# Relation pass of a graph network: SP fetches one chunk in 64 row by row, GpSimd the others without the padding

## What is computed

```python
# layer 1 (relation pass), h = layernorm(x)
msg = h[edge_src] * edge_norm[:, None]
agg = segment_sum(msg, edge_rel * N + edge_dst)          # 8 relations
out = einsum('rnbi,rbio->nbo', agg, W)                   # 8 blocks of 32 x 32
# layer 3 (attention pass)
alpha = leaky_relu(a_src[src] + a_dst[dst]); w = softmax of alpha over each dst
out = segment_sum(xp[src] * w, dst)
```

## Time and profile before

| | |
|---|---|
| median of 3 runs | 7745.9 us (7744.19 to 7753.85) |
| the profiled execution | 7754.0 us |
| its span, first to last instruction | 7752.0 us |
| stage 1 (up to the first gather) | 0 to 387.5 us |
| relation pass, first gather to last add | 387.5 to 2943.5 us |
| attention pass, first to last gather | 3668.7 to 6536.6 us |
| mean granted clock of PE over the span | 0.716 of full speed |

### The profile page before, as it was taken

How to read it: one execution, slowest core, us unless ns; L and a number is a source line. 1 busy time by engine, 2 the same in 40 slices (tenths; PEclk the granted TensorE clock), 3 DMA queues, 4 the chain that set the end, 5 groups by cost and what they waited for, 6 DMA issues and landing times. The chain is left out here.

```text
span 7752.0 us, 114430 instructions
## 1 busy us (share of the span) xinstructions
PE 5127.6 (66%) x25073; PEld 4291.3 (55%) x25073; DVE 4010.3 (52%) x11854; ACT 1970.2 (25%) x4898; POOL 4204.7 (54%) x4656
## 2 busy tenths in 40 slices
PE   9935555555555558697355656565655656769999
PEld 4424455454545546596344445454544545659998
DVE  5534444444444448523555555555555556764443
ACT  3300000000000005232232333332322333436666
POOL 1166666666666655355655555555555554654444
PEclk9967666666666679798566666666556566559999
DMA  8833333333333327112432333333333332644444
GB/s 310 314 91 87 88 87 87 87 87 87 87 87 87 87 78 241 66 63 88 117 87 78 88 87 82 87 86 82 86 82 82 84 86 66 200 147 71 71 71 67
DMA packets 378112, 797.65 MB, mean 103 GB/s; under 512 B 88994, under 2 KB 234994, under 8 KB 364692
## 3 DMA queue, kind: packets, MB, share of 16 engines
q0 software_dynamic: 209712, 525.20, 26.1%
q1 hardware_dynamic: 140724, 154.25, 6.4%
q10 hardware_dynamic: 27440, 116.02, 4.0%
HBM read 565.73 MB, written 229.43 MB: 103 GB/s over the span
## 5 line engine op out<-in xcount | busy, mean ns | idle before, releaser
L1274 POOL DMA_INDIRECT s_rows<-xp_table,s_index x1664 | 1593.2, 957 | 1276.0 <-DVE s_scaled L1562 768.1
L1397 PE MATMUL s_part<-s_pick,s_scaled 128*128 128x128 f32 x6656 | 1603.9, 404 | 949.5 <-DVE s_scaled L1562 650.4
L373 PE MATMUL s_part<-s_pick,s_rows 128*128 128x128 f32 x6656 | 1444.8, 382 | 1114.5 <-DVE s_pick L381 685.4
L347 POOL DMA_INDIRECT s_rows<-rel_table,s_staged x1664 | 1580.7, 950 | 929.6 <-issue 432.6
L1397 PEld LDWEIGHTS s_part<-s_pick,s_scaled 128*128 128x128 f32 x6656 | 1330.7, 289 | 1187.8 <-DVE sums L1577 681.4
L373 PEld LDWEIGHTS s_part<-s_pick,s_rows 128*128 128x128 f32 x6656 | 1231.6, 270 | 1328.3 <-DVE s_pick L381 818.5
L394 DVE TENSOR_TENSOR sums<-sums,s_part 128x256 f32 x1666 | 702.6, 422 | 1237.8 <-issue 689.8
L1577 DVE SCALAR_TENSOR_TENSOR sums<-sums,s_old_share,s_part 128x256 f32 x1666 | 795.6, 478 | 1051.1 <-DMA s_rows<-rel_table,s_staged 540.1
L1310 ACT ACTIVATE s_apart<-window,s_local 128x128 f32<-128x128 f32 x1664 | 531.6, 390 | 1854.7 <-PE s_part L1397 1362.8
L1562 DVE TENSOR_TENSOR s_scaled<-s_rows,s_psW 128x256 f32<-128x256 f32 x1664 | 678.5, 408 | 69.7 <-issue 69.7
L381 DVE TENSOR_SCALAR s_pick<-window,s_local,s_weight 128x128 f32<-128x128 f32 x1669 | 595.4, 357 | 157.3 <-issue 105.5
(11 more groups left out here) (356 smaller groups left out, 5423.2 us busy)
## 6 DMA issues: line engine op xcount, KB each, us to landing
rel_table<-s_rows ACTq DMA_DIRECT2D x98, 1024.0 KB
s_rows<-exp_rows SPq DMA_DIRECT2D x212, 132.0 KB
s_rows<-rel_table,s_staged POOLq DMA_INDIRECT x1664
s_rows<-xp_table,s_index POOLq DMA_INDIRECT x1664
s_edges<-edge_rows SPq DMA_DIRECT2D x208, 80.0 KB
xp_table<-s_xp ACTq DMA_DIRECT2D x49, 264.0 KB, 3.9
s_x<-in_x SPq DMA_DIRECT2D x98, 128.0 KB
s_x<-in_x SPq DMA_DIRECT2D x49, 256.0 KB
```

The source lines that it names most:

```text
L347: pool.indirect_dma_start(out=rows[:, s, :], out_offset=None, in_=rel_table[:, :], in_offset=bass.IndirectOffsetOnAxis(ap=staged[:, 2 * s ...
L373: mm = pe.matmul(part[s % PARTS][:, k, :], rows[:, s, k * P:(k + 1) * P], pick[:, s % PICKS, :], start=True, stop=True)
L1274: pool.indirect_dma_start(out=rows[:, b * BATCH + s, :], out_offset=None, in_=xp_table[0:NR, :], in_offset=bass.IndirectOffsetOnAxis(ap=in ...
L1397: mm = pe.matmul(part[s % 4][:, k, :], scaled[:, s % SCALED, k * P:(k + 1) * P], pick[:, s % (2 * GRP), :], start=True, stop=True)
```

## The change

SP gets slot 63 of every round. To have its row numbers in order, stage 1 copies every 64th column of `index` (26 of them) on DVE, PE transposes them, DVE copies them to `lists`; SP stores these to memory (`fetch_lists`) at the begin of the pass. For a round SP loads one list of 128 numbers to one partition (`list_now`), waits until PE has used slot 63 of the round before, reads the numbers into registers, four to a load, and issues for each a transfer of one row of 1 KB to its partition: 32 loads and 128 transfers a round. The rows count on two semaphores in turn, and PE waits for both at slot 63. The list of the next round is loaded after the last register load of this one.

POOL leaves out slot 63, and of the last round the chunks from 1661 on (slots 61 and 62), and in the attention pass the three padding chunks. For this the last round of POOL and PE and the last iteration of POOL in the attention pass are written out behind their loops.

```diff
+FILLED = -(-E // P)
+FOUR = 4
@@ stage 1, DVE, at the end
+                    def own_chunks():
+                        v.wait_ge(edges_done, 1)
+                        v.tensor_copy(own[:, :], index[:, SLOTS - 1:CHUNKS:SLOTS]).then_inc(own_ready, 1)
...
+                    v.wait_ge(own_turned, 1)
+                    v.tensor_copy(lists[:, :], psI[0:CHUNKS // SLOTS, :])
@@ stage 1, PE, at the end
+                    pe.wait_ge(own_ready, 1)
+                    pe.transpose(psI[0:CHUNKS // SLOTS, :], own[:, :], ident[:, :]).then_inc(own_turned, 1)
@@ relation pass, SP: new
+                    def load_list(i):
+                        sp.dma_start(list_now[:, :], fetch_lists[ds(i, 1), :]).then_inc(list_in, 16)
+
+                    def fetch(i, more):
+                        sp.wait_ge(list_in, 16 * i + 16)
+                        sp.sem_inc(fetch_go, 1)
+                        for j in range(0, P, FOUR):
+                            _, from_rows = nc.values_load_multi_w_load_instructions(
+                                list_now[0:1, j:j + FOUR], engines=[mybir.EngineType.SP], min_val=0, max_val=R * NR - 1,
+                                skip_runtime_bounds_check_because="a source times eight plus a type, both in range")
+                            if more and j + FOUR == P:
+                                load_list(i + 1)
+                            for k, from_row in enumerate(from_rows):
+                                sp.dma_start(rows[j + k:j + k + 1, SLOTS - 1, :], rel_table[ds(from_row, 1), :]).then_inc(fetched[k % 2], 16)
+
+                    sp.dma_start(fetch_lists, lists[:, :]).then_inc(lists_out, 16)
+                    sp.wait_ge(lists_out, 16)
+                    load_list(0)
+                    fetch(0, True)
+                    with sp.Fori(1, ROUNDS2 - 1) as i:
+                        sp.wait_ge(product, SLOTS * i + 2)
+                        fetch(i, True)
+                    sp.wait_ge(product, SLOTS * (ROUNDS2 - 1) + 2)
+                    fetch(ROUNDS2 - 1, False)
@@ relation pass, ACT
-                                act.wait_ge(gathered[g], 16 * GRP * i)
+                                act.wait_ge(gathered[g], 16 * (GRP if g < GROUPS - 1 else GRP - 1) * i)
@@ relation pass, POOL
+                            if s == SLOTS - 1 or isinstance(i, int) and i * SLOTS + s >= FILLED:
+                                continue
@@ relation pass, PE
-                                pe.wait_ge(gathered[s // GRP], 16 * GRP * i + 16 * GRP)
+                                by_pool = GRP if s + GRP < SLOTS else GRP - 1
+                                pad = max(0, c + by_pool - FILLED) if isinstance(i, int) else 0
+                                pe.wait_ge(gathered[s // GRP], 16 * by_pool * i + 16 * (by_pool - pad))
+                            if s == SLOTS - 1:
+                                for k in range(2):
+                                    pe.wait_ge(fetched[k], 16 * P // 2 * i + 16 * P // 2)
@@ attention pass, POOL
-                                gather(s, b)
+                                if not isinstance(i, int) or (2 * i + b) * BATCH + s < FILLED:
+                                    gather(s, b)
@@ attention pass, ACT
-                        act.wait_ge(gathered[b], LANDED * i + LANDED)
+                        pad = max(0, (2 * i + b + 1) * BATCH - FILLED) if isinstance(i, int) else 0
+                        act.wait_ge(gathered[b], LANDED * i + LANDED - 16 * pad)
```

More of the change, by code:

```diff
@@ L93, in gnn_kernel @@
     edge_rows = dram("edge_rows", [CHUNKS, 5, P])
+    fetch_lists = dram("fetch_lists", [CHUNKS // SLOTS, P], I32)
     whole_rows = dram("whole_rows", [BATCHES, HEADS * BATCH])
@@ L160, in gnn_kernel @@
         local = at(gather_of, "s2_local", [P, CHUNKS + AHEAD])
+        lists = at(gather_of, "s2_lists", [CHUNKS // SLOTS, P], I32)
         weight = at(gather_of, "s2_weight", [P, CHUNKS + AHEAD])
@@ L175, in gnn_kernel @@
             psT = [bank(st, f"s1_psT{b}", HALVES, P) for b in range(2)]
+            psI = bank(st, "s1_psI", P)
+            own = at(st, "s1_own", [P, CHUNKS // SLOTS])
+            own_ready, own_turned = sem("s1_own_ready"), sem("s1_own_turned")
             psO = [bank(st, f"s1_psO{k}", R * P, banks=2) for k in range(HALVES)]
@@ L261, in step @@
                             pair_nodes()
+                            own_chunks()
                     norm(0, 0, 0)
                     by_tiles(v, step)
+                    v.wait_ge(own_turned, 1)
+                    v.tensor_copy(lists[:, :], psI[0:CHUNKS // SLOTS, :])
                 @block.scalar
@@ L315, in gnn_kernel @@
             pick = at(st, "s2_pick", [P, PICKS, P])
+            list_now = at(st, "s2_list_now", [1, P], I32)
+            lists_out, list_in, fetch_go = sem("s2_lists_out"), sem("s2_list_in"), sem("s2_fetch_go")
+            fetched = [sem(f"s2_fetched{k}") for k in range(2)]
             part = [bank(st, f"s2_part{k}", HALVES, P) for k in range(PARTS)]
@@ L324, in gnn_kernel, with _ @@
             with nc.Block() as block:
+                @block.sync
+                def _(sp):
+                    def load_list(i):
[20 more added lines that the diff above has]
+                    fetch(ROUNDS2 - 1, False)
                 @block.scalar
@@ L355, in _, with later_round @@
                             gathers(0, g, True)
-                    with pool.Fori(1, ROUNDS2) as i:
+                    def later_round(i):
                         for b in range(2):
@@ L360, in _, with combine_round @@
                                 gathers(i, g, False)
+                    with pool.Fori(1, ROUNDS2 - 1) as i:
+                        later_round(i)
+                    later_round(ROUNDS2 - 1)
                 @block.tensor
                 def _(pe):
-                    pe.sem_inc(product, 2)
-                    with pe.Fori(0, ROUNDS2) as i:
+                    def combine_round(i):
                         for s in range(SLOTS):
@@ L375, in _ @@
                             mm.then_inc(product, 1)
+                    pe.sem_inc(product, 2)
+                    with pe.Fori(0, ROUNDS2 - 1) as i:
+                        combine_round(i)
+                    combine_round(ROUNDS2 - 1)
                 @block.vector
@@ L1297, in _ @@
                         gather(s, 1)
-                    with pool.Fori(1, BATCHES // 2) as i:
+                    with pool.Fori(1, BATCHES // 2 - 1) as i:
                         gathers(i, 0)
                         gathers(i, 1)
+                    gathers(BATCHES // 2 - 1, 0)
+                    gathers(BATCHES // 2 - 1, 1)
                 @block.scalar
```

## The result

The kernel after takes 8566.2 us (median of 4 runs, 8544.6 to 8587.1) against 7745.4 us before (4 runs): a ratio of 1.1056, interval 1.1043 to 1.1069, 821 us slower. The forecast was 7726 us with a range up to 8150. The profiled execution of the kernel after took 8587.1 us, that of before 7754.0.

What follows compares the result with a forecast made beforehand. It took the relation pass to be paced by POOL's gather runs slowing DVE's queue, then POOL pausing at a full ring. Terms -31 + 13 + 0 - 2 = -20 us from 7745.9 gave 7726 us, range 7700 to 8150.

Steps and rivals of the forecast that it cites:

- Fewer gathers, 31 us: Relation pass: POOL's omitted gathers save 1.25 us in each of 25 rounds, 31 us; bounds 0 and 42 us.
- SP's chain, 73 us a round: Relation pass: SP's 32 groups of one four-number load and four row transfers take 2.29 us each; bounds 70 and 113.
- Rival 2: Register loads on SP cost number by number: 7741 us at 2.75 us per four rows (0.06), 7980 at 3.2 (0.10).
- The cover, 96.5 us: Relation pass: SP's chain plus landing, 75 us, hides within a whole round of 96.5 us, with 20 to spare.
- Rival 1: Relation pass: slow stretches beside gathers hit SP's queue too, +11 us a round, 8036 us; chance 0.31.
- The share 0.46: Relation pass: DVE's queue is slow for 46% of the time, from 0.93 us a chunk fast, 5.1 slow, 1.50 mean.
- The last round, +13 us: Relation pass: the last round's cover is only 62 us, so 13 us of SP's chain and landing are paid.
- The first round free: Relation pass: SP's first fetch costs nothing, starting about 395 us while PE reaches the round's end at 561.7 us.
- DMA, 0: Relation pass: 128 more descriptors a round on SP's queue replace a gather of the same bytes; engines 31% busy, cost nothing.
- Stage 1, 0: Before the relation pass: the added copies and transpose hide in 5 us of cover; zero, or 1 us without it.
- Attention pass, -2: Attention pass: three padding gathers fewer count only in the last batch, saving 0 to 3.8 us, taken as 2.
- Rival 3: Relation pass: POOL's saved time was idle anyway and becomes pause, leaving the last round's 13 us, 7757 us; chance 0.06.

## Why the prediction was wrong

*Fewer gathers, 31 us.* Right in its mechanism, a little small: 1.6 us a round in the run with the slot left out, over the upper bound of 1.50; the forecast took 1.25. On the second kind of chip, where POOL is the bound, 28 gathers fewer at 1.25 give 35 us; 37 were measured.

*SP's chain, 73 us a round.* Right in itself: 72.5 us in the last round, 2.27 us for four rows instead of 2.29. The parts were off and made up for each other: the load 555 ns instead of 268 and the 152 of what waits for it, the transfer 225 instead of 260. Rival 2 (7741 or 7980 us) is out.

*The cover, 96.5 us, "75 us fit with 20 to spare".* This step failed. It set the duration of a chain whose queue runs undisturbed against a stretch in which gathers run. Beside them the chain needs 125.7 us and PE stands 32.6 us a round, where the forecast had no wait before the last round.

*Rival 1.* The mechanism is this one, at +11 us a round and 8036 us; it was +33.4. The step that was mis-sized is the rate of 0.66 = 0.54 + 0.46/3.7. The share 0.46 was worked out from DVE's chunks, and taken over for SP. By the rows of the kernel after: PE waits 32.6 us of the 129.9, and POOL stands still then too; less 2 for the landing, SP works 30 us there at its full speed (in the tenth of the later rounds POOL's last gather starts at 1849.7 us, and the trace has none of SP's slow instructions from 1852 to the end of the chain at 1880.6). So it did 72.5 - 30 = 42 us of its work in the other 95, a rate of 0.45. With the slow stretch 3.7 times as long that would be a slow share of 0.75, an estimate. DVE's chunk is in good part work of its engine, which the stretches don't touch; SP's chain is queue instructions and nothing else, and its own chain lengthens DVE's stretches too. The range's end of 8150 us varied the chain by 5 us and left the rate alone. The rate's own bound, slow all the time, is 1/3.7 = 0.27: 26 us of work done beside gathers, 46 left over, a round of 143 us and some 8900 us, which would have held the result.

*The last round, +13 us.* Right for PE, from 62.2 us to 75.8, but only 8 of it reach the end of the pass: before, DVE's last add came 6 us after PE's last matmul (2945.3 against 2939.2 us), and now it comes less than 1 us after (3777.6 against 3776.9). *The first round free.* Wrong: it ends 22 us later. POOL fills the empty ring, 123 gathers in the first 203 us, and SP needs 191 us for its first chain (390.2 to 581.3 us).

*DMA, 0.* Nothing speaks against it. *Stage 1, 0.* Right: the first gather starts at 387.6 us against 387.5. *Attention pass, -2.* It doesn't show: what lies behind the last add is 4806.7 us before and 4807.8 after, and on the second kind of chip 4024.4 after and 4022.3 to 4027.0 in the four kernels with all gathers. *Rival 3* is out.

*The chance.* The forecast gave the mechanism that decided 0.31 and its own 0.42; slower it had at 0.46 in all and faster at 0.36, so its number, that of the likeliest single case, lay on the less likely side. Against rival 1 stood that the queues of PE and ACT show no such stretch. That is true, and for PE it stayed true. It was no witness for another queue in new work, as the run with ACT showed.

*What stays open:* what it is in a gather that holds up the queues of other engines, and why two chips are free of it. Shown is: it takes gathers by POOL (plain loads at a higher DMA share don't do it); it hits SP, DVE in the relation pass and ACT when it fetches, not PE, nor ACT in the attention pass; it depends on the gathers' pace and on what else the queues issue; and the chips differ in it with the same program. A rule of the Trainium skill (Perfetto Trace Analysis, DMA Optimizations) says that balancing transfers across the engines that can issue them may help where the bottleneck is making descriptors. On the second kind of chip, where POOL with its gathers is the bound, the measurement agrees, 0.57% faster. On the first POOL is not the bound, it waits for PE, so the rule's condition isn't met, and the same move costs 10.6%.

## What to carry to other kernels

An engine that seems idle is not free: before a chain of small instructions is put on its queue, look in the trace for the maxima of such instructions on any queue beside the same neighbours, and price the whole chain at the slow rate as the bound. Another queue that stays fast there is no witness that this one will: ACT's was fast beside gathers in one pass and slow when it fetched rows in the other. On the first kind of chip, moving a gather's rows to another queue would have been worth it only if the chain fitted into the round at less than half its speed and a gather were worth more than the 2 us or so that even a hidden chain cost. A gain or loss found on one chip is to be repeated on another.

## What the runs showed of the hardware that was not expected

- The kernel before takes 7697 to 7783 us on three chips and 6506 to 6512 us on two. In the kernel after, SP's MOVE is 2 to 1402 ns on one and 29 ns throughout on the other.
- Pauses make POOL's gathering quicker on the first kind (one run): 1499 gathers with a memset of 0.33 us behind each, in the time of 1461 without.
- A register load of four numbers lasts 555 ns and one of one number 495 ns on SP's queue; a one-row transfer of 1 KB keeps that queue 225 ns, and 229 on ACT's.
- A gather of POOL is followed by 0.30 us of idle time. A memset of 0.11 us fits into it, and the gathers still follow each other every 1.25 us.
- Beside gathers that slow DVE's and SP's queues, 1600 register instructions of ACT's queue in the attention pass never exceed 51 ns, and 1638 instructions of PE's in the relation pass never exceed 36.
